# Moving the pair sums of a two-layer attention kernel to GpSimd, with a larger share of the subtraction on VectorE and the subtraction one group later

## The chip, the cores and the metric

The kernel runs on one core of a Trainium2 chip. The metric is the device time of one execution in microseconds (us).

## The reference

A float32 image of 2 x 512 x 48 x 48 goes through two layers, each an attention with a residual. Layer 0 normalises in 32 groups first and has biases; layer 1 adds a position embedding to the input of queries and keys. Both have 8 heads of 64 channels over 2304 positions:

```python
scores = jnp.einsum('bhqd,bhkd->bhqk', q, k) * scale
attn = jax.nn.softmax(scores, axis=-1)
o = jnp.einsum('bhqk,bhkd->bhqd', attn, v)
o = o.transpose(0, 2, 1, 3).reshape(B, S, HEADS * hd_v)
o = o @ Wout + bout
```

## The kernel before

The program is written as raw queues: each engine has its own list of instructions, and semaphores order them. The stages follow each other: group norm, projections of layer 0, attention of layer 0, output projection and projections of layer 1, attention of layer 1, output projection. The change touches `attention_stage` alone, which runs once per layer.

An attention stage has NB = 48 blocks: 2 images x 4 pairs of heads x 6 chunks of 384 queries. A block has 18 key tiles of 128 keys, in KC = 6 groups of three, c = 0 to 5. Every engine runs the same software pipeline: `body(t, par)` walks the six steps of block t, and in step c each engine also does work for earlier groups. `behind(t, par, c, lag)` gives the block and group that lie `lag` steps back.

What happens to a group, in steps after its scores:
- TensorE, `scores` (L681): scores of both heads for each of the three key tiles, into three pairs of PSUM banks (k = 0, 1, 2). `bank_free` waits until ScalarE has copied the bank's last contents.
- VectorE, `maximum` (L860): running maximum over the key tiles, from PSUM and a running buffer. ScalarE, `copy` (L755): the scores from PSUM into `prob`, after the maximum. After step 5 VectorE folds the two running maxima (`fold_slots`, L866).
- In step 0 of the next block TensorE transposes the fold (`turn`, L651), VectorE reduces it (L847), and in step 1 TensorE broadcasts the maxima (L658) and ScalarE copies them to `mx` (L763).
- Lag 7, `shift` (L589): `prob - mx`, columns 0 to 207 of 384 on VectorE, 208 to 383 on GpSimd. GpSimd waits for VectorE's part of the same group.
- Lag 9, `exponential` (L771) on ScalarE, two instructions for the two heads, after both parts.
- Lag 10, `weigh` (L692): TensorE multiplies the exponentials with the values, into bank 6. Lag 10 too, `pair_tiles` (L872): VectorE adds two of the three key tiles of a group into `two_tiles`, so that the key sums need fewer products.
- Lag 11, `add_keys` (L708): TensorE sums over the keys with a matrix of ones, into bank 7, from `two_tiles` and the third tile.
- Then, for a finished block: ScalarE copies the weighted sums in step 3 (`copy_weighted`, L777) and the denominators in step 5 (`copy_den`, L783), TensorE transposes the denominators in step 2 of the next block (`turn_den`, L665), VectorE sums and inverts them (L889, L895), ScalarE widens (L789), TensorE spreads them in step 3 (L671), VectorE multiplies (`norm`, L905) and ScalarE's queue stores.

On TensorE's queue a step is: transposes if the step has any, scores, `weigh`, `add_keys`. On VectorE's: three maxima with what is interleaved, the fold, the pair, the subtraction. On ScalarE's: three copies, two exponentials with what is interleaved. GpSimd has its part of the subtraction alone. For the last block of a stage VectorE subtracts all 384 columns and the key sums take all three tiles.

Of the kernel before, what the change touches and what calls it, by code (L numbers as in the profile page):

```python
# [6 lines left out]
ALU = mybir.AluOpType  # L7
# [18 lines left out]
SCALE = float(D) ** -0.5  # L26
GN_EPS = 1e-5
NORM_STEPS = 10
SHIFT_DVE = 208
SHIFT_LAG, EXP_LAG, PV_LAG, PAIR_LAG, DEN_LAG = 7, 9, 10, 10, 11  # L30
TURN_AT, BROADCAST_AT = 0, 1
PV_COPY_AT, DEN_COPY_AT, DEN_TURN_AT, DEN_SPREAD_AT, STORE_AT = 3, 5, 2, 3, 3


def is_block(t, *numbers):
# [478 lines left out]
def attention_stage(nc, name, psum, bufs, qk_d, v_d, att_d, next_loads):  # L514
# [6 lines left out]
    with ExitStack() as ctx:  # L521
        def sem(n):
            return ctx.enter_context(nc.semaphore(f"{name}_{n}"))
# [17 lines left out]
        dve_shifted, pool_shifted = sem("dve_shifted"), sem("pool_shifted")  # L541
        exp_done = sem("exp_done")
        paired = sem("paired")
        pv_done = sem("pv_done")
        den_copied, pv_copied = sem("den_copied"), sem("pv_copied")
        den_turned, den_summed, inverted = sem("den_turned"), sem("den_summed"), sem("inverted")
        widened, spread = sem("widened"), sem("spread")
# [83 lines left out]
        def _(pe):  # L631
# [3 lines left out]
            def bank_free(t, c, k):  # L635
                if c > 0 or not before(t, 1):
                    pe.wait_ge(copied, slot(t, 3 * (c - 1) + k) if live(t) else slot(NB - 1, KT - 1))
                if c == BROADCAST_AT + 1 and not before(t, 1) and live(t - 1):
                    pe.wait_ge(mx_ready, 3 * (t - 1) + k + 1)

            def spare_free(t, c):
                if c == DEN_TURN_AT + 1 and not before(t, 3) and live(t - 3):
# [42 lines left out]
            def weigh(t, par, c):  # L685
                if c == 0 and not before(t, 1):
                    pe.wait_ge(pv_copied, t)
                pe.wait_ge(v_in[c], 16 * (t // JB + 1))
                pe.wait_ge(exp_done, 2 * group(t, c))
                for kt in range(3 * c, 3 * c + 3):  # L690
                    for d in range(0, P, 32):
                        mm = nc.tensor.matmul(psum[d:d + 32, 6, 0:CH], vst[:, kt, d:d + 32],  # L692
                                              prob[par][:, d // D, kt, :], start=(kt == 0), stop=(kt == KT - 1),
                                              tile_position=(0, d))
                return mm

            def add_keys(t, par, c):
                if c == 0 and not before(t, 1):
                    pe.wait_ge(den_copied, t)
                if last(t):  # L700
                    rounds = [[prob[par][:, e, 3 * c + i, :] for e in range(2) for i in tiles] for tiles in ((0, 1), (2,))]
                else:
                    pe.wait_ge(paired, group(t, c))
                    rounds = [[x for e in range(2) for x in (two_tiles[c % 2][:, e, :], prob[par][:, e, 3 * c + 2, :])]]
                for n, tiles in enumerate(rounds):
                    for i, tile in enumerate(tiles):
                        r = i * P // len(tiles)
                        mm = nc.tensor.matmul(psum[r:r + 32, 7, 0:CH], ones[:, :], tile, start=(c == 0 and n == 0),  # L708
                                              stop=(c == KC - 1 and (n == len(rounds) - 1 or r % D > 0)), tile_position=(0, r))
                return mm  # L710

            def body(t, par):
                for c in range(KC):
                    spare_free(t, c)
                    if c == TURN_AT and not before(t, 1) and live(t - 1):
                        bank_free(t, c, 2)
                        turn(t - 1)
                    if c == BROADCAST_AT and not before(t, 1) and live(t - 1):
                        bank_free(t, c, 2)
                        broadcast_max(t - 1)  # L720
                    if c == DEN_TURN_AT and not before(t, 3) and live(t - 3):
                        bank_free(t, c, 2)
                        turn_den(t - 3)
                    if c == DEN_SPREAD_AT and not before(t, 3) and live(t - 3):
                        bank_free(t, c, 2)
                        spread_den(t - 3)
                    if live(t):
                        for k in range(3):
                            bank_free(t, c, k)
                            scores(t, par, c, k)  # L730
                    tv, pv, cv = behind(t, par, c, PV_LAG)
                    td, pd, cd = behind(t, par, c, DEN_LAG)
                    mm = None
                    if live(tv):
                        mm = weigh(tv, pv, cv)
                    if live(td):
                        mm = add_keys(td, pd, cd)
                    if mm is not None:
                        mm.then_inc(pv_done, 1)

            blocks(pe, body)

# [1 line left out]
        def _(act):  # L744
            def copy(t, par, s):
                c, k = divmod(s, 3)
                if s < 2:
                    act.wait_ge(scored, scored_count(slot(t, s)))
                else:
                    act.wait_ge(maxed, maxed_count(t, s))  # L750
                if c == TURN_AT and not before(t, 1):
                    act.wait_ge(reduced, 3 * (t - 1) + k + 1)
                if not before(t, 2):
                    act.wait_ge(pv_done, pv_count(t - 2, c + 1))
                nc.scalar.activation(prob[par][:, :, s, :], s_banks(k)[:, :, 0:CH], ACT.Copy).then_inc(copied, 1)  # L755

            def copy_max(t, par, r):
# [13 lines left out]
                nc.scalar.activation(x, x, ACT.Exp, scale=SCALE).then_inc(exp_done, 1)  # L771

            def copy_weighted(t):
                act.wait_ge(pv_done, pv_count(t, KC - 1))
                if not before(t, 1):
                    act.wait_ge(normed, 3 * t)
                nc.scalar.activation(pvr[:, :], pv_bank, ACT.Copy).then_inc(pv_copied, 1)  # L777

            def copy_den(t):
                act.wait_ge(pv_done, pv_count(t, KC))  # L780
                if not before(t, 1):
                    act.wait_ge(den_turned, t)
                nc.scalar.activation(den[:, :], den_bank, ACT.Copy).then_inc(den_copied, 1)  # L783
# [16 lines left out]
            def body(t, par):  # L800
                for c in range(KC):
                    te, pe_, ce = behind(t, par, c, EXP_LAG)
                    if c == DEN_COPY_AT and not before(t, 2) and live(t - 2):
                        copy_den(t - 2)
                    for k in range(3):
                        if k == 2 and c == DEN_TURN_AT and not before(t, 3) and live(t - 3):
                            widen(t - 3)
                        if live(t):
                            copy(t, par, 3 * c + k)
                        if c == BROADCAST_AT and not before(t, 1) and live(t - 1):  # L810
                            copy_max(t - 1, 1 - par, k)
                    for e in range(2):
                        if live(te):
                            exponential(te, pe_, ce, e)
                        if e == 0 and c == PV_COPY_AT and not before(t, 2) and live(t - 2):
                            copy_weighted(t - 2)
                    if c == STORE_AT and not before(t, 3) and live(t - 3):
                        store(t - 3, 1 - par)

# [3 lines left out]

        @block.gpsimd
        def _(pool):
            def body(t, par):
                for c in range(KC):
                    if c == 0:
# [1 line left out]
                    pool.wait_ge(copied, slot(t, 3 * c + 2))  # L830
                    pool.wait_ge(dve_shifted, group(t, c))
                    shift_part(nc.gpsimd, par, c, SHIFT_DVE, CH).then_inc(pool_shifted, 1)

            with pool.Fori(0, NB // 2 - 1) as it:
                for par in range(2):
                    body(2 * it + par, par)
            body(NB - 2, 0)

        @block.vector
        def _(dve):  # L840
# [21 lines left out]
            def fold_slots(t):  # L862
# [1 line left out]
                if not before(t, 1):  # L864
                    dve.wait_ge(turned, t)
                nc.vector.tensor_tensor(fold[:, :, :], run[0][:, :, :], run[1][:, :, :], ALU.max).then_inc(folded, 1)  # L866

            def pair_tiles(t, par, c):
                dve.wait_ge(exp_done, 2 * group(t, c))
                if c >= 2 or not before(t, 1):  # L870
                    dve.wait_ge(pv_done, pv_count(t, c - 1))
                nc.vector.tensor_tensor(two_tiles[c % 2][:, :, :], prob[par][:, :, 3 * c, :],  # L872
                                        prob[par][:, :, 3 * c + 1, :], ALU.add).then_inc(paired, 1)

            def shift(t, par, c):
                if c == 0:
# [30 lines left out]
            def body(t, par):  # L907
                for c in range(KC):
# [10 lines left out]
                            maximum(t, par, 3 * c + k)  # L919
                    if c == KC - 1 and live(t):  # L920
                        fold_slots(t)
                    tp, pp, cp = behind(t, par, c, PAIR_LAG)
                    if live(tp) and not last(tp):
                        pair_tiles(tp, pp, cp)
                    ts, ps, cs = behind(t, par, c, SHIFT_LAG)
                    if live(ts):
                        shift(ts, ps, cs)
# [171 lines left out]
```

## Time and profile before

| | |
|---|---|
| median of 3 runs | 4300.96 us (4295.68 to 4301.03) |
| profiled execution, its own time | 4301.96 us |
| its span, first to last instruction | 4300.2 us |
| granted TensorE clock, mean | 0.992 |
| TensorE busy with products | 4097.7 us (95%) |
| VectorE busy | 3211.7 us (75%) |
| ScalarE busy | 2815.7 us (65%) |
| GpSimd busy | 1408.7 us (33%) |
| DMA, mean over the span | 48 GB/s |

The busy times are of the whole span, which has four stages without attention work in it; within the attention stages VectorE and ScalarE are busier than these shares say. Matmuls are pipelined and their ends are modelled, so a busy TensorE may still have rests between steps. The clock is in parts of full speed.

### The profile page before, as it was taken

The page shows a single profiled execution, that of the slowest core. Times are in us where ns is not written, and L with a number is a line of the kernel's source. Part 1 is how long each engine was busy: PE and PEld are TensorE (multiplying, and loading weights), DVE is VectorE, ACT ScalarE, POOL GpSimd, SP SyncE. Part 2 cuts the span into 40 slices and gives each one's busy share as a digit, 9 for nine tenths or more (in the row PEclk, how much of TensorE's full clock was granted, in tenths as well). Part 3 has the DMA queues.
Part 4 walks back from the last instruction along what each step waited for, and adds up shares of the span by engine and source line. Part 5 has one row for each costly group of instructions (what it writes and reads, how often), then busy time and mean ns, then how long its engine had stood idle before and what let it go on. Part 6 is the DMA issues. An engine that isn't in the chain of part 4 may idle for free. (4 is left out here: it accounts for less than half of the span.)

```text
span 4300.2 us, 88739 instructions
## 1 busy us (share of the span) xinstructions
PE 4097.7 (95%) x30024; PEld 1912.0 (44%) x30024; DVE 3211.7 (75%) x4032; ACT 2815.7 (65%) x3557; POOL 1408.7 (33%) x572
## 2 busy tenths in 40 slices
PE   7998999999999999998999989999999999999989
PEld 4554444444444444444555544444444444444445
DVE  3112899999999999997322239999999999999962
ACT  1112788888888888886000018888888888888850
POOL 0000444444444444443100004444444444444410
PEclk9999999999999999999999999999999999999999
DMA  4122000101000000011323320100000000000116
GB/s 173 73 80 86 8 28 18 35 13 31 21 26 22 22 24 24 26 48 41 124 101 124 105 84 9 35 15 31 18 27 24 22 22 24 26 20 29 41 45 212
DMA packets 157934, 208.42 MB, mean 48 GB/s; under 512 B 9009, under 2 KB 144305, under 8 KB 156849
## 3 DMA queue, kind: packets, MB, share of 16 engines
q1 hardware_dynamic: 137712, 179.28, 12.7%
q10 hardware_dynamic: 20160, 28.32, 1.8%
q8 instruction: 39, 0.64, 0.1%
q14 instruction: 23, 0.18, 0.0%
HBM read 113.19 MB, written 94.37 MB: 48 GB/s over the span
## 5 line engine op out<-in xcount | busy, mean ns | idle before, releaser
L589 POOL TENSOR_TENSOR prob<-prob,mx 128x1056 f32<-128x1056 f32 x564 | 1387.7, 2460 | 2675.9 <-DVE prob L589 2675.9
L755 ACT ACTIVATE prob<-psum_att 128x768 f32<-128x768 f32 x1728 | 1393.3, 814 | 967.9 <-PE psum_att L681 539.4
L681 PE MATMUL psum_att<-qst,kst 64*128 64x384 f32 x6912 | 1288.3, 504 | 26.8 <-DMA kst<-qk_scratch 17.9
L692 PE MATMUL psum_att<-prob,vst 128*32 128x384 f32 x13824 | 1239.9, 491 | 77.3 <-ACT prob L771 77.2
L771 ACT ACTIVATE prob<-prob 128x1152 f32<-128x1152 f32 x1152 | 1285.6, 1164 | 0.0
L860 DVE TENSOR_TENSOR run<-psum_att,run 128x768 f32<-128x768 f32 x1344 | 1234.0, 950 | 11.9 <-PE psum_att L681 2.7
L589 DVE TENSOR_TENSOR prob<-prob,mx 128x1248 f32<-128x1248 f32 (+1 forms) x576 | 853.5, 1483 | 65.4 <-ACT mx L763 65.4
L681 PEld LDWEIGHTS psum_att<-qst,kst 64*128 64x128 f32 x6912 | 624.0, 188 | 530.7 <-ACT prob L755 152.3
L692 PEld LDWEIGHTS psum_att<-prob,vst 128*32 128x32 f32 x13824 | 396.1, 109 | 834.9 <-issue 573.3
L872 DVE TENSOR_TENSOR two_tiles<-prob 128x768 f32<-128x768 f32 x564 | 559.0, 991 | 0.4 <-ACT prob L771 0.4
L309 PE MATMUL psum<-xc_l,wq 128*128 128x384 f32 x1536 | 504.0, 489 | 10.1 <-DVE qk_l L406 5.0
L708 PE MATMUL psum_att<-prob,const_sb 128*32 128x384 f32 x2400 | 483.5, 487 | 0.0
L708 PE MATMUL psum_att<-two_tiles,const_sb 128*32 128x384 f32 x2256 | 465.0, 487 | 0.0
L309 PEld LDWEIGHTS psum<-xc_l,wq 128*128 128x128 f32 x1536 | 293.8, 191 | 220.9 <-issue 20.3
L860 DVE TENSOR_TENSOR run<-psum_att,prob 128x768 f32<-128x768 f32 x192 | 183.6, 957 | 100.4 <-PE psum_att L681 100.4
L350 ACT ACTIVATE qk_l<-psum,par_sb 128x384 f32<-128x384 f32 x96 | 55.7, 580 | 309.1 <-PE psum L309 309.1
L176 PE MATMUL psum<-attc_l,wo_l 128*128 128x384 f32 x768 | 252.5, 490 | 3.3 <-PEq L521 3.3
L424 DVE TENSOR_TENSOR vo_l<-psum,bv 128x512 f32<-128x512 f32 x36 | 24.9, 692 | 308.5 <-PE psum L326 308.5
L708 PEld LDWEIGHTS psum_att<-two_tiles,const_sb 128*32 128x32 f32 x2256 | 140.4, 110 | 217.2 <-issue 217.2
L176 PEld LDWEIGHTS psum<-attc_l,wo_l 128*128 128x128 f32 x768 | 147.2, 192 | 106.0 <-issue 5.8
L406 DVE TENSOR_TENSOR qk_l<-psum,emb_table 128x384 f32<-128x384 f32 x96 | 53.2, 557 | 187.2 <-PE psum L309 187.2
L708 PEld LDWEIGHTS psum_att<-prob,const_sb 128*32 128x32 f32 x2400 | 146.9, 110 | 8.2 <-issue 7.7
(55 smaller groups left out, 1596.3 us busy)
## 6 DMA issues: line engine op xcount, KB each, us to landing
qk_scratch<-qk_l SPq DMA_DIRECT2D x48, 768.0 KB, 3.5
v_scratch<-vo_l SPq DMA_DIRECT2D x24, 768.0 KB, 3.5
qst<-qk_scratch SPq DMA_DIRECT2D x96, 192.0 KB, 2.4
kst<-qk_scratch SPq DMA_DIRECT2D x96, 192.0 KB, 2.4
vst<-v_scratch SPq DMA_DIRECT2D x96, 192.0 KB, 2.5
att_scratch<-ob ACTq DMA_DIRECT2D x96, 192.0 KB, 1.9
attc_l<-att_scratch SPq DMA_DIRECT2D x24, 768.0 KB, 5.4
x_sb<-in_x SPq DMA_DIRECT2D x8, 1152.0 KB, 13.9
```

The costliest lines, as they stand in the source:

```text
L176: mm = nc.tensor.matmul(bank, w[c], att[:, c, :], start=(c == 0), stop=(c == CT - 1))
L309: mm = nc.tensor.matmul(qk_bank(m), qkv["w"][:, c, m * P:(m + 1) * P], xc[p][:, c, :], start=(c == 0), stop=(c == CT - 1))
L350: nc.scalar.activation(qk[half][:, mt, :], qk_bank(m), ACT.Identity, bias=bias[:, m:m + 1])\
L406: nc.vector.tensor_tensor(qk[half][:, mt, :], qk_bank(m), emb_of(i, m), ALU.add)\
L589: return engine.tensor_tensor(x, x, m, ALU.subtract)
L681: mm = nc.tensor.matmul(psum[:, 2 * k + e, 0:CH], kst[rows, (3 * c + k) * P:(3 * c + k + 1) * P], qst[par][rows, :], start=True, stop=True ...
L692: mm = nc.tensor.matmul(psum[d:d + 32, 6, 0:CH], vst[:, kt, d:d + 32], prob[par][:, d // D, kt, :], start=(kt == 0), stop=(kt == KT - 1), ...
L708: mm = nc.tensor.matmul(psum[r:r + 32, 7, 0:CH], ones[:, :], tile, start=(c == 0 and n == 0), stop=(c == KC - 1 and (n == len(rounds) - 1 ...
L755: nc.scalar.activation(prob[par][:, :, s, :], s_banks(k)[:, :, 0:CH], ACT.Copy).then_inc(copied, 1)
L771: nc.scalar.activation(x, x, ACT.Exp, scale=SCALE).then_inc(exp_done, 1)
L860: nc.vector.tensor_tensor(r[:, :, :], s_banks(s % 3)[:, :, 0:CH], other, ALU.max).then_inc(maxed, 1)
L872: nc.vector.tensor_tensor(two_tiles[c % 2][:, :, :], prob[par][:, :, 3 * c, :], prob[par][:, :, 3 * c + 1, :], ALU.add).then_inc(paired, 1)
```

## The change

Constants: VectorE's share of the subtraction goes from 208 to 304 of 384 columns, GpSimd's from 176 to 80. The subtraction is 8 steps behind the scores instead of 7, `weigh` 11 instead of 10, `add_keys` stays at 11, the exponential at 9 and the pair at 10. The finished block's steps move: both copies to step 4, the transpose of the denominators to 3, the spread and the store to 4. `pair_tiles` goes from VectorE's queue to GpSimd's, behind the subtraction of the same step (which is of the group two later); it still waits for the exponentials and for the key sums that last read its buffer. `weigh` has a semaphore of its own, so that the weighted sums can be copied before the key sums of that step.

```diff
-SHIFT_DVE = 208
-SHIFT_LAG, EXP_LAG, PV_LAG, PAIR_LAG, DEN_LAG = 7, 9, 10, 10, 11
+SHIFT_DVE = 304
+SHIFT_LAG, EXP_LAG, PAIR_LAG, PV_LAG = 8, 9, 10, 11
 TURN_AT, BROADCAST_AT = 0, 1
-PV_COPY_AT, DEN_COPY_AT, DEN_TURN_AT, DEN_SPREAD_AT, STORE_AT = 3, 5, 2, 3, 3
+PV_COPY_AT, DEN_TURN_AT, DEN_SPREAD_AT, STORE_AT = 4, 3, 4, 4
...
+                if c > BROADCAST_AT + 1 and not live(t) and live(t - 1):
+                    pe.wait_ge(mx_ready, 3 * t)
...
-                return mm
+                if c == KC - 1:
+                    mm.then_inc(weighed, 1)
...
-                return mm
+                mm.then_inc(pv_done, 1)
...
                     tv, pv, cv = behind(t, par, c, PV_LAG)
-                    td, pd, cd = behind(t, par, c, DEN_LAG)
-                    mm = None
                     if live(tv):
-                        mm = weigh(tv, pv, cv)
-                    if live(td):
-                        mm = add_keys(td, pd, cd)
-                    if mm is not None:
-                        mm.then_inc(pv_done, 1)
+                        weigh(tv, pv, cv)
+                        add_keys(tv, pv, cv)
...
                 if not before(t, 2):
-                    act.wait_ge(pv_done, pv_count(t - 2, c + 1))
+                    act.wait_ge(pv_done, pv_count(t - 2, c))
...
             def copy_weighted(t):
-                act.wait_ge(pv_done, pv_count(t, KC - 1))
+                act.wait_ge(weighed, t + 1)
...
             def copy_den(t):
-                act.wait_ge(pv_done, pv_count(t, KC))
+                act.wait_ge(pv_done, pv_count(t, KC - 1))
...
-                    if c == DEN_COPY_AT and not before(t, 2) and live(t - 2):
-                        copy_den(t - 2)
...
                         if e == 0 and c == PV_COPY_AT and not before(t, 2) and live(t - 2):
                             copy_weighted(t - 2)
+                    if c == PV_COPY_AT and not before(t, 2) and live(t - 2):
+                        copy_den(t - 2)
...
         @block.gpsimd
         def _(pool):
+            def pair_tiles(t, par, c):
+                pool.wait_ge(exp_done, 2 * group(t, c))
+                if c >= 2 or not before(t, 1):
+                    pool.wait_ge(pv_done, pv_count(t, c - 2))
+                nc.gpsimd.tensor_tensor(two_tiles[c % 2][:, :, :], prob[par][:, :, 3 * c, :],
+                                        prob[par][:, :, 3 * c + 1, :], ALU.add).then_inc(paired, 1)
+
...
                     shift_part(nc.gpsimd, par, c, SHIFT_DVE, CH).then_inc(pool_shifted, 1)
-
-            with pool.Fori(0, NB // 2 - 1) as it:
-                for par in range(2):
-                    body(2 * it + par, par)
-            body(NB - 2, 0)
+                    tp, pp, cp = behind(t, par, c, PAIR_LAG - SHIFT_LAG)
+                    if live(tp):
+                        pair_tiles(tp, pp, cp)
+
+            body(0, 0)
+            with pool.Fori(0, (NB - 2) // 2) as it:
+                for p in range(2):
+                    body(2 * it + 1 + p, 1 - p)
+            for c in range(KC - PAIR_LAG + SHIFT_LAG, KC):
+                pair_tiles(NB - 2, 0, c)
...
-            def pair_tiles(t, par, c):
-                dve.wait_ge(exp_done, 2 * group(t, c))
-                if c >= 2 or not before(t, 1):
-                    dve.wait_ge(pv_done, pv_count(t, c - 1))
-                nc.vector.tensor_tensor(two_tiles[c % 2][:, :, :], prob[par][:, :, 3 * c, :],
-                                        prob[par][:, :, 3 * c + 1, :], ALU.add).then_inc(paired, 1)
...
-                    tp, pp, cp = behind(t, par, c, PAIR_LAG)
-                    if live(tp) and not last(tp):
-                        pair_tiles(tp, pp, cp)
```

## Rows read from the trace of the kernel before

**Rows 1.** Window 500 to 1950: busy of PE, PEld, DVE, ACT, POOL; clock.
```profile
500.00:1950.00 1450.00, 1399.19 (x12378) 612.81 (x12372) 1360.02 (x1668) 1259.09 (x1582) 646.80 (x263) 1.00 0.08 26
```

**Rows 2.** Waits, 1000 to 1900: us in total, times, longest.
```profile
PE psum_att L692 <- ACT prob L771: 19.1, 27, 0.7
```

**Rows 3.** Timeline of TensorE, one block (steps 2, 3, 4, 5, 0, 1).
```profile
1002.87 2.21 PE L681 MATMUL psum_att<-qst,kst 64*128 64x384 f32 x12
...
1006.97 0.49 PE L708 MATMUL psum_att<-two_tiles,const_sb 128*32 128x384 f32 x1
...
1007.88 0.55 PE L671 MATMUL psum_att<-const_sb,dwide 128*128 128x128 f32 x3
1008.36 2.21 PE L681 MATMUL psum_att<-qst,kst 64*128 64x384 f32 x12
...
1013.22 2.21 PE L681 MATMUL psum_att<-qst,kst 64*128 64x384 f32 x12
1016.13 2.14 PE L692 MATMUL psum_att<-prob,vst 128*32 128x384 f32 x24 [0.71 <-ACT prob L771]
1018.85 2.21 PE L681 MATMUL psum_att<-qst,kst 64*128 64x384 f32 x12
...
1023.73 0.85 PE L651 MATMUL psum_att<-const_sb,fold 128*128 128x128 f32 x6
1024.51 2.21 PE L681 MATMUL psum_att<-qst,kst 64*128 64x384 f32 x12
...
1030.16 2.21 PE L681 MATMUL psum_att<-qst,kst 64*128 64x384 f32 x12
...
1035.45 0.55 PE L665 MATMUL psum_att<-const_sb,den 128*128 128x128 f32 x3 [0.37 <-ACT mx L763]
1035.93 2.21 PE L681 MATMUL psum_att<-qst,kst 64*128 64x384 f32 x12
```

**Rows 4.** Timeline of VectorE in the same block: a subtraction, pairs, the fold.
```profile
1002.47 1.46 DVE L589 TENSOR_TENSOR prob<-prob,mx 128x1248 f32<-128x1248 f32 x1 [0.69 <-ACT mx L763]
...
1006.90 0.95 DVE L872 TENSOR_TENSOR two_tiles<-prob 128x768 f32<-128x768 f32 x1
...
1012.67 0.95 DVE L872 TENSOR_TENSOR two_tiles<-prob 128x768 f32<-128x768 f32 x1
...
1022.62 0.96 DVE L866 TENSOR_TENSOR fold<-run 128x768 f32<-128x768 f32 x1
...
1027.98 1.19 DVE L872 TENSOR_TENSOR two_tiles<-prob 128x768 f32<-128x768 f32 x1
...
1033.88 0.95 DVE L872 TENSOR_TENSOR two_tiles<-prob 128x768 f32<-128x768 f32 x1
```

**Rows 5.** Timeline of ScalarE in the same block: copies, and the den copy.
```profile
1007.02 0.81 ACT L755 ACTIVATE prob<-psum_att 128x768 f32<-128x768 f32 x1
...
1012.78 0.81 ACT L755 ACTIVATE prob<-psum_att 128x768 f32<-128x768 f32 x1 [0.25 <-DVE run L860]
...
1015.97 2.46 ACT L755 ACTIVATE prob<-psum_att 128x768 f32<-128x768 f32 x3
...
1020.43 0.48 ACT L783 ACTIVATE den<-psum_att 128x384 f32<-128x384 f32 x1
```

**Rows 6.** Groups by line and form, 700 to 2000, and one instruction of GpSimd.
```profile
L589 POOL TENSOR_TENSOR prob<-prob,mx 128x1056 f32<-128x1056 f32 x235 | 578.2, 2460 | 716.1 <-DVE prob L589 716.1
...
L589 DVE TENSOR_TENSOR prob<-prob,mx 128x1248 f32<-128x1248 f32 x235 | 341.2, 1452 | 26.9 <-ACT mx L763 26.9
...
1004.01 2.47 POOL L589 TENSOR_TENSOR prob<-prob,mx 128x1056 f32<-128x1056 f32 x1 [4.01 <-DVE prob L589]
```

**Rows 7.** Both engines at once: timeline; the table sum's min/median/max ns.
```profile
4121.79 2.47 POOL L589 TENSOR_TENSOR prob<-prob,mx 128x1056 f32<-128x1056 f32 x1 [3.53 <-DVE prob L589]
4122.56 2.52 DVE L872 TENSOR_TENSOR two_tiles<-prob 128x768 f32<-128x768 f32 x1
...
L228 POOL TENSOR_TENSOR emb_table<-emb_parts x4: 4047/5208/6429, 2036.9 to 2051.4; 128x2304 f32<-128x2304 f32 x4
```

More of the change, by code:

```diff
@@ L543, in attention_stage @@
         paired = sem("paired")
-        pv_done = sem("pv_done")
+        weighed, pv_done = sem("weighed"), sem("pv_done")
         den_copied, pv_copied = sem("den_copied"), sem("pv_copied")
```

## The prediction

> **What bounds the kernel now.** I read the busy windows first, then the waits, then the timelines of one block on all engines. Over a steady attention stretch TensorE is busy 1399 of 1450 us, VectorE 1360, ScalarE 1259, GpSimd 647, at a granted clock of 1.00 [rows 1]. TensorE sets the pace, with VectorE close behind, and its products stand still in two places only, once a block each: 27 times 0.7 for the exponential in 900 us [rows 2], and 0.37 behind the copy of the maximum [rows 3]. The reader should see that the most to be won is TensorE's rest, not VectorE's work.
>
> A block has six steps c = 0 to 5 and takes 33.06 us (1035.93 - 1002.87) [rows 3]. A step without anything extra takes 4.86 (1008.36 to 1013.22). The key sums of a step begin 4.10 after its scores (1006.97 - 1002.87). The transposes add 0.48 (den turn), 0.48 (spread), 0.78 (turn) and 0.79 (broadcast: 5.65 from 1024.51 to 1030.16, less 4.86), together 2.53. So TensorE needs 6 x 4.86 + 2.53 = 31.69, and 1.37 is waiting: 0.43 before the den turn (1035.45 against 1030.16 + 4.86), 0.15 before the spread (1007.88 against 1007.73), 0.77 in step 4, whose value products wait for the second exponential, and 0.02 before the turn. There are 45 such blocks a layer (I count 45 even intervals between the turns), 90 in all: the waiting is worth 90 x 1.37 = 123 us and no more.
>
> **The change part by part.**
> Subtraction a step later, value products a step later (lag 11). The exponential of a group is then two steps old when its products come; the 0.77 goes. What is late next in that place is the copy of the weighted sums, which had ended 0.28 before the weigh would have wanted it. The den turn moves from step 2 to step 3: it no longer follows the three copies of the maximum, which ended just before it, and the copies of step 2 have no widening or den sums among them. The 0.43 goes. VectorE's wait for the maximum (0.69 a block [rows 4]) goes too, but VectorE was not the bound there. The spread and the three normalisations move from step 3 to 4, behind the widening in step 3: I take the same 0.15 for the spread as now (its bank's last copy starts 4.15 after the step's start and ends at 4.96 [rows 5]; spread at 5.01).
>
> ScalarE, steps 4 and 5. Both copies, weighted and den, now fall into step 4, together with the normalisations that make its copies late. By today's step 3: the third copy starts 4.42 after the step's start (1012.78 - 1008.36); from there to the next step's first copy are 3.19 (copy, exponential, weighted copy, exponential), then 0.48 for the den copy that today comes a step later, then three copies in 2.46 [rows 5]. They end at 10.55, the turn can go at 10.60, and TensorE would want it at 9.72. New wait: 0.88. So part of what was won is lost one step later, before the turn.
>
> VectorE. 768 elements take 0.95 and 1248 take 1.45 [rows 4, 6], a slope of 1.05 ns and 0.15 fixed. The subtraction of 304 columns has 1824 elements: 1.45 + 576 x 1.05 = 2.05, 0.60 more. The pair, 0.87 from start to start, goes. VectorE wins 0.27 a step; nothing on the path gains by it, as TensorE is the pace.
>
> GpSimd. It subtracts 80 columns (480 elements) and adds pairs (768). The only row like it is 1056 elements in 2.46 [rows 6]. With a fixed part f, both together take P = 2.91 + 0.82 f. Bounds: f = 0 gives 2.91 (if the plain pair went at the rate of the embedding table's sum, 4.05 for 2304 [rows 7], P would be 2.47); a line through 1056 in 2.46 and 2304 in 4.05 gives f = 1.1 and P = 3.82. I take f = 0.15, as VectorE's own, P = 3.03: the nearest row is the subtraction itself, the table's sum has another pattern.
>
> The exclusion between the two. A VectorE operation with both inputs in SBUF doesn't run beside GpSimd: one pair addition that began 1.70 before the end of GpSimd's subtraction took 2.52 instead of 0.95, 1.57 more, while the table sum took GpSimd 6.43 instead of 4.05 where VectorE was first [rows 7]. So I charge the overlap less 0.13. The maxima, with an input in PSUM, stay at 0.95 beside GpSimd. The Trainium skill says the same (SBUF — State Buffer, "Who interferes with whom": a VectorE instruction with two SBUF inputs contends with a GpSimd one that reads SBUF, and the second blocks until the first is done); the trace agrees, 1.57 for 1.70, and it speaks against giving GpSimd more. In this kernel it matters now: GpSimd starts 0.08 after the subtraction ends (1004.01 for 1003.93 [rows 4, 6]), and the next one begins 2.6 later at the earliest.
>
> The new chain: subtraction of step c, GpSimd's part, its pair, then the key sums of step c+1, which stand before the next scores on TensorE's queue, so every delay there is TensorE's. Pairs are ready 2.05 + 0.08 + P + 0.06 = 2.19 + P after the subtraction's start. Its place after a step's start is where the pair stands today: 3.72 in step 1, 4.03 with den sums, 4.31 with normalisations, 3.47 in step 0 [rows 3, 4].
> - Step 2's sums: wanted at 4.86 + 4.10 = 8.96 from step 1's start, ready at 5.91 + P: late from P = 3.05.
> - Step 3's: the subtraction of step 2 starts at 8.59, is held 0.03, pairs at 13.84, wanted at 14.30. Step 4's: ready at S3 + 4.03 + 5.22 = 9.25, wanted at 5.49 + 4.10 = 9.59. Both in time.
> - Step 5's: ready at 4.31 + 5.22 = 9.53 from step 4's start, wanted at 8.96: 0.57 late, but within the 0.88 of ScalarE's copies. The fold (two SBUF inputs) stands at 8.89, is held by the pair to end at 7.27 + P = 10.30: also within it. Up to P = 3.28 this costs nothing more.
> - Step 0's: that subtraction starts at S4 + 7.19 + P, pairs ready at 2P - 2.00 after step 0's start, wanted at 4.10: late from P = 3.05, by twice the excess. The subtraction of step 0 is held about 0.4, which the next step takes up.
>
> Sum, P = 3.03: step 1 4.86; step 2 with den turn 5.34; step 3 to 4 5.01 + 0.48 = 5.49; to the turn 10.60 and 0.78; step 0 with broadcast 5.65: 32.72, against 33.06. 0.34 x 90 = 31 us. Fill and drain change by one step in which VectorE sets the pace; I put them at 0, within 5 us either way. The profiled execution is 4301.96 (span 4300.2 and 1.8 around it), 1.0 over the median 4300.96: 4301 - 31 = 4270.
>
> **The rivals.**
> Slower: GpSimd is dearer. Above 3.05 the block grows by 3 (P - 3.05), so it is even at P = 3.16, f = 0.31, only 0.13 over my value. With the table sum's rate as slope (1.76 ns), f = 0.60 and P = 3.40: 1.05 + 0.12 (step 5) more, 33.89, +0.83 x 90 = 75 us: 4376. At P = 3.82 the block is about 35.6: 4530. For it: no row shows GpSimd's fixed part, and the one other size is cheaper per element, as with a large f. Against: its pattern repeats both operands.
>
> No change: P between 3.12 and 3.20 (f 0.25 to 0.35), where the gain of 31 and the lateness of the pairs cancel; at 3.14 the block is 32.99, 6 us won: 4295. The GpSimd page of the skill (GPSIMD Engine Reference, "Elementwise — side-by-side cycle accounting") gives 4497 ns for 2048 elements; a line through that and the row's 2460 would give just this P, an estimate, and so 4295; no run here shows that size.
>
> All waiting gone: if the copies of steps 4 and 5 fit (VectorE 0.27 a step earlier, den copy behind other waits), 31.69 a block, 4301 - 123 = 4178; half of it 4225. Against: ScalarE's chain is made of operations back to back.
>
> **How the numbers follow.** Forecast 0.50 (4262 to 4285), more gained 0.08, no change 0.12, slower 0.30. Within 0.2% is about what a measurement can't tell from no change. Faster 0.58, same 0.12, slower 0.30. The range 4225 to 4395 goes from half the waiting gone to a little over the slope case, leaving 0.05 below and 0.13 above.
>
> **What would show it.** After the change: block 32.7; no wait of the value products for the exponential in step 4 and of the den turn; a wait of 0.8 to 0.9 before the turn, put down to ScalarE's copy; POOL 1.20 and 1.83; VectorE's subtraction 2.05, about 2.5 in step 0 and the fold about 1.4. TensorE waiting for GpSimd's pair in steps 0 and 2 would be the slower rival. The prediction is wrong if GpSimd's two take over 3.16, if the lock lets VectorE in between them, or if a drain grows by more than 5 us.

## The result and the profile after

The changed kernel takes 4267.54 us (median of 4, 4265.96 to 4270.81) against 4300.66 before: ratio 0.9927, 95% interval 0.9909 to 0.9944, 33 us less. The forecast was 4270.

The lines have moved in the changed kernel: scores L683, value products L694, key sums L711, turn L653, broadcast L660, den turn L667, spread L673, maximum L870, fold L876, GpSimd's pair L828, ScalarE's copies L753.

Busy windows of the changed kernel, the same stretch as in [rows 1] and the same columns:

```profile
500.00:1950.00 1450.00, 1425.85 (x12546) 608.52 (x12542) 1342.85 (x1424) 1253.63 (x1602) 801.79 (x535) 1.00 0.08 25
```

TensorE is now busy 1426 of 1450 us instead of 1399, GpSimd 802 instead of 647, VectorE 17 us less. The reader should see that the gain is TensorE's rest and no more. By these windows it is 27 us of it; by the length of the blocks below it is 0.44 x 44.5 = 20, and as the ends of products are modelled, the blocks are the better measure.

Waits of the changed kernel, 1000 to 1900 (total, times, longest):

```profile
PEld psum_att L711 <- POOL two_tiles L828: 40.5, 111, 0.6
...
PE psum_att L711 <- POOL two_tiles L828: 12.8, 28, 0.5
```

The two waits of before, for the exponential (27 times 0.7, [rows 2]) and behind the maximum's copy, are not there. One new one is: the key sums wait 0.46 for GpSimd's pair, once a block (PE is the products, PEld the loading of their weights). It shows in the timeline (TensorE, steps 4, 5, 0, 1, 2, 3 and the next 4; compare [rows 3]):

```profile
1001.95 2.21 PE L683 MATMUL psum_att<-qst,kst 64*128 64x384 f32 x12
...
1006.81 2.21 PE L683 MATMUL psum_att<-qst,kst 64*128 64x384 f32 x12
1008.94 2.14 PE L694 MATMUL psum_att<-prob,vst 128*32 128x384 f32 x24
1011.54 0.48 PE L711 MATMUL psum_att<-two_tiles,const_sb 128*32 128x384 f32 x1 [0.46 <-POOL two_tiles L828]
...
1012.36 0.85 PE L653 MATMUL psum_att<-const_sb,fold 128*128 128x128 f32 x6
1013.14 2.21 PE L683 MATMUL psum_att<-qst,kst 64*128 64x384 f32 x12
...
1017.31 0.51 PE L711 MATMUL psum_att<-two_tiles,const_sb 128*32 128x384 f32 x1
...
1018.89 2.21 PE L683 MATMUL psum_att<-qst,kst 64*128 64x384 f32 x12
...
1023.75 2.21 PE L683 MATMUL psum_att<-qst,kst 64*128 64x384 f32 x12
...
1029.08 2.21 PE L683 MATMUL psum_att<-qst,kst 64*128 64x384 f32 x12
...
1034.09 0.55 PE L673 MATMUL psum_att<-const_sb,dwide 128*128 128x128 f32 x3
1034.57 2.21 PE L683 MATMUL psum_att<-qst,kst 64*128 64x384 f32 x12
```

The block is 32.62 (1034.57 - 1001.95) where it was 33.06. Step by step against the prediction: step 4 to the turn 10.41 (10.60 predicted), turn 0.78 (0.78), step 0 5.75 (5.65), step 1 4.86 (4.86), step 2 with den turn 5.33 (5.34), step 3 with spread 5.49 (5.49). The waits are 0.69 before the turn, 0.15 before the spread and 0.10 in step 0: 0.93 instead of 1.37.

This is layer 0. In layer 1 every second block of the changed kernel is 0.11 longer (32.72 and 32.61 in turn): the third maximum of its step 3 starts 0.21 after the reciprocal and not 0.11 (3021.63 after 3021.42, 3054.24 after 3054.13), and the copy and the spread behind it are as late. The kernel before and the version with the lags alone don't have it, every version with the later lags and the pairs on GpSimd does. Its cause stays open; it is worth some 2 us.

VectorE, GpSimd and ScalarE in step 5 of the same block (compare [rows 4, 5]):

```profile
1008.22 2.68 DVE L870 TENSOR_TENSOR run<-psum_att,run 128x768 f32<-128x768 f32 x3
1010.94 1.27 DVE L876 TENSOR_TENSOR fold<-run 128x768 f32<-128x768 f32 x1
1012.14 2.04 DVE L589 TENSOR_TENSOR prob<-prob,mx 128x1824 f32<-128x1824 f32 x1
...
1008.38 1.22 POOL L589 TENSOR_TENSOR prob<-prob,mx 128x480 f32<-128x480 f32 x1 [2.76 <-DVE prob L589]
1009.55 1.84 POOL L828 TENSOR_TENSOR two_tiles<-prob 128x768 f32<-128x768 f32 x1
...
1009.56 0.49 ACT L781 ACTIVATE den<-psum_att 128x384 f32<-128x384 f32 x1
1009.93 2.22 ACT L753 ACTIVATE prob<-psum_att 128x768 f32<-128x768 f32 x3
```

The pair ends at 1011.39, the key sums begin at 1011.54 (wanted at 1006.81 + 4.10 = 1010.91) and the turn follows them 0.82 later. The last copy ends at 1012.15, the fold, held by the pair, at 1012.21, and the turn stands at 1012.36. Which of the three is last? In all ten profiles of this case the turn stands 0.14 or 0.15 behind the end of the fold, whatever the key sums and the copies do. Late key sums in other steps (vector_256, move_only) are followed by the next transposes after 0.78 to 0.79, and the spread stands 0.05 behind the end of its bank's copy. By these the key sums would allow the turn at 1012.32 and the copies at 1012.20. So the fold is last, the key sums 0.04 and the copies 0.16 before it, and the fold and the key sums both hang on the end of GpSimd's pair.

The groups by form, 700 to 1950 (compare [rows 6]):

```profile
L589 DVE TENSOR_TENSOR prob<-prob,mx 128x1824 f32<-128x1824 f32 x230 | 500.1, 2174 | 0.0
...
L828 POOL TENSOR_TENSOR two_tiles<-prob 128x768 f32<-128x768 f32 x231 | 425.2, 1841 | 0.0
L589 POOL TENSOR_TENSOR prob<-prob,mx 128x480 f32<-128x480 f32 x230 | 278.1, 1209 | 558.2 <-DVE prob L589 558.2
...
L876 DVE TENSOR_TENSOR fold<-run 128x768 f32<-128x768 f32 x38 | 48.5, 1277 | 1.3
```

GpSimd's two take 1.21 and 1.84; as the second starts 1.17 after the first, P is 3.01. VectorE's subtraction is 2.05 at the median (2.05 + 0.12 on average, what the exclusion costs it), the fold 1.28 instead of 0.96.

### The profile page after: what moved, and what is told of

It is laid out like the page before. It is cut to its first block and busy times, and to the rows that moved or that the text cites. A ratio compares the mean times of both kernels' runs of the same rounds, so it can differ in the third digit from the quotient of the medians.

```text
span 4264.2 us, 88501 instructions
## 1 busy us (share of the span) xinstructions
PE 4117.6 (97%) x30024; PEld 1882.8 (44%) x30024; DVE 3141.5 (74%) x3468; ACT 2773.2 (65%) x3557; POOL 1727.9 (41%) x1136
## 5 line engine op out<-in xcount | busy, mean ns | idle before, releaser
L753 ACT ACTIVATE prob<-psum_att 128x768 f32<-128x768 f32 x1728 | 1360.7, 822 | 970.9 <-PE psum_att L683 559.3
L589 POOL TENSOR_TENSOR prob<-prob,mx 128x480 f32<-128x480 f32 x564 | 690.0, 1223 | 2335.8 <-DVE prob L589 2335.8
L683 PE MATMUL psum_att<-qst,kst 64*128 64x384 f32 x6912 | 1288.8, 505 | 29.6 <-DMA kst<-qk_scratch 17.8
L870 DVE TENSOR_TENSOR run<-psum_att,run 128x768 f32<-128x768 f32 x1344 | 1234.3, 950 | 56.7 <-PE psum_att L683 42.8
L589 DVE TENSOR_TENSOR prob<-prob,mx 128x1824 f32<-128x1824 f32 (+1 forms) x576 | 1264.4, 2196 | 3.6 <-ACT mx L761 3.6
L694 PE MATMUL psum_att<-prob,vst 128*32 128x384 f32 x13824 | 1241.6, 491 | 0.4 <-issue 0.4
L828 POOL TENSOR_TENSOR two_tiles<-prob 128x768 f32<-128x768 f32 x564 | 1041.2, 1846 | 0.0
L683 PEld LDWEIGHTS psum_att<-qst,kst 64*128 64x128 f32 x6912 | 623.4, 188 | 533.7 <-ACT prob L753 101.8
L694 PEld LDWEIGHTS psum_att<-prob,vst 128*32 128x32 f32 x13824 | 394.1, 109 | 754.3 <-issue 702.7
L711 PE MATMUL psum_att<-two_tiles,const_sb 128*32 128x384 f32 x2256 | 469.0, 490 | 51.9 <-POOL two_tiles L828 51.8
L711 PE MATMUL psum_att<-prob,const_sb 128*32 128x384 f32 x2400 | 490.4, 491 | 0.0
L870 DVE TENSOR_TENSOR run<-psum_att,prob 128x768 f32<-128x768 f32 x192 | 182.8, 953 | 108.6 <-PE psum_att L683 108.6
L711 PEld LDWEIGHTS psum_att<-two_tiles,const_sb 128*32 128x32 f32 x2256 | 115.0, 109 | 325.8 <-issue 174.8
L857 DVE TENSOR_REDUCE mcol<-psum_att 128x2 f32<-128x256 f32 x288 | 122.0, 425 | 44.9 <-PE psum_att L683 38.7
```

The lines of the kernel that those rows point to most:

```text
L589: return engine.tensor_tensor(x, x, m, ALU.subtract)
L683: mm = nc.tensor.matmul(psum[:, 2 * k + e, 0:CH], kst[rows, (3 * c + k) * P:(3 * c + k + 1) * P], qst[par][rows, :], start=True, stop=True ...
L828: nc.gpsimd.tensor_tensor(two_tiles[c % 2][:, :, :], prob[par][:, :, 3 * c, :], prob[par][:, :, 3 * c + 1, :], ALU.add).then_inc(paired, 1)
L857: nc.vector.tensor_reduce(mcol[:, :, r], s_banks(r)[:, :, CH:512], AX.X, ALU.max).then_inc(reduced, 1)
L870: nc.vector.tensor_tensor(r[:, :, :], s_banks(s % 3)[:, :, 0:CH], other, ALU.max).then_inc(maxed, 1)
```

## The experiments

The two theories: (1) what was won is TensorE's two waits, by the later value products and the later den turn, and the move of the pairs to GpSimd is a cost; (2) what was won is VectorE's relief. All times below are medians of 4 with the ratio to the kernel before on the same chip (it took 4300.28 and 4299.69 us beside the two sets of runs).

**lags_only.** The changed kernel, the pairs back on VectorE ahead of its subtraction, 208 columns.

```diff
-SHIFT_DVE = 304
+SHIFT_DVE = 208
...
-                    if live(tp):
-                        pair_tiles(tp, pp, cp)      # on GpSimd
...
+                    tp, pp, cp = behind(t, par, c, PAIR_LAG)
+                    if live(tp) and not last(tp):
+                        pair_tiles(tp, pp, cp)      # on VectorE
```

> The later subtraction, value products, copies and den turn alone; pairs stay on VectorE and the subtraction at 208 columns. Theory 1 (the gain is the later value products and den turn, 0.77 and 0.43 us a block; the move to GpSimd is a cost): a block of 32.3 to 32.4 us, only the spread's 0.15 and about 0.5 before the turn left as waits; 4240 us, faster than the changed kernel's 4268. Theory 2 (the gain is VectorE's relief): nothing much won, 4290 to 4301.

Measured 4244.28 (4243.20 to 4245.75), ratio 0.987 [0.9853, 0.9886]. Half the change is faster than the whole. TensorE's timeline, a turn, step 4's scores and the next turn; and VectorE's fold:

```profile
1009.98 0.85 PE L653 MATMUL psum_att<-const_sb,fold 128*128 128x128 f32 x6 [0.58 <-DVE fold L864]
...
1032.08 2.21 PE L683 MATMUL psum_att<-qst,kst 64*128 64x384 f32 x12
...
1042.44 0.85 PE L653 MATMUL psum_att<-const_sb,fold 128*128 128x128 f32 x6 [0.58 <-DVE fold L864]
...
1041.33 0.96 DVE L864 TENSOR_TENSOR fold<-run 128x768 f32<-128x768 f32 x1
```

The block is 32.46 (1042.44 - 1009.98). Here the turn stands 10.36 after step 4's start and waits for the fold: VectorE, with the pair, sets that place. No key sums wait. Theory 1 holds; theory 2 falls.

This also prices the move to GpSimd. The fold starts 9.25 after step 4's start here (1041.33 - 1032.08) and 8.99 in the changed kernel: VectorE's relief makes it 0.26 earlier. But there the pair holds it for 0.31, and step 0 is 0.10 longer: 0.16 a block in all. Of the 21.0 us between the two profiled spans 16.7 lie between the even turns, layer 1's longer blocks included; the other 4.3 are in fill and drain.

**move_only.** The other half: the kernel before with `SHIFT_DVE = 304` and the pairs on GpSimd's queue, three steps behind its subtraction, all lags and places as before.

```diff
-SHIFT_DVE = 208
+SHIFT_DVE = 304
...
+                    tp, pp, cp = behind(t, par, c, PAIR_LAG - SHIFT_LAG)
+                    if live(tp):
+                        pair_tiles(tp, pp, cp)      # on GpSimd, PAIR_LAG 10, SHIFT_LAG 7
...
-                    tp, pp, cp = behind(t, par, c, PAIR_LAG)
-                    if live(tp) and not last(tp):
-                        pair_tiles(tp, pp, cp)      # on VectorE
```

> The other half: pairs on GpSimd and 304 columns on VectorE, all lags and places as in the kernel before. Theory 1: the three waits of the kernel before stay, and the key sums of step 2 come late by some 0.7 us, as the subtraction of the step before waits for the maximum; a block of 33.7, 4355 us, slower than before. Theory 2: 4265 to 4280, as VectorE has 0.27 us a step less to do.

Measured 4368.99 (4368.02 to 4370.02), ratio 1.0159 [1.0142, 1.0176]. Its TensorE timeline (lines as in the kernel before) has the old waits and a new one; the block is 33.76 (1037.08 - 1003.32):

```profile
1003.32 0.85 PE L651 MATMUL psum_att<-const_sb,fold 128*128 128x128 f32 x6
...
1015.15 0.55 PE L665 MATMUL psum_att<-const_sb,den 128*128 128x128 f32 x3 [0.37 <-ACT mx L763]
...
1020.41 0.51 PE L708 MATMUL psum_att<-two_tiles,const_sb 128*32 128x384 f32 x1 [0.51 <-POOL two_tiles L830]
...
1029.44 2.14 PE L692 MATMUL psum_att<-prob,vst 128*32 128x384 f32 x24 [0.71 <-ACT prob L771]
...
1037.08 0.85 PE L651 MATMUL psum_att<-const_sb,fold 128*128 128x128 f32 x6
```

The key sums of step 2 stand 0.68 late, as expected, and the block is 0.70 longer; that is 63 of the 69 us, and the time is 14 above the 4355 expected.

The two halves, -56 and +69 us, don't add up to -33, which is 46 less than their sum. Here VectorE's subtraction waits 1.56 for the maximum once a block (27 times between 1000 and 1900, 42.0 us), and that makes the pair late in step 2; with the later subtraction that wait is gone. The lags are worth more where the pairs are on GpSimd.

**vector_336.** The changed kernel with `SHIFT_DVE = 336`.

> The changed kernel with 336 columns on VectorE instead of 304: VectorE's subtraction 2.25 instead of 2.05, GpSimd's 0.80 instead of 1.21, the chain from the subtraction's start to the pair 0.2 shorter. Theory 1 (the pair sets the wait before the turn): that wait falls from 0.69 to 0.5, the 0.10 of step 0 goes; a block of 32.33, 4242 us. Rival (ScalarE's copies set it, as predicted): 4266 to 4275, as VectorE's longer subtraction only makes the copies later.

Measured 4246.71 (4243.76 to 4248.69), ratio 0.9877 [0.9861, 0.9894]. **vector_320**, `SHIFT_DVE = 320`:

> The changed kernel with 320 columns on VectorE. Theory 1: at 304 the key sums set the turn (10.4 after step 4's start), at 336 sums, fold and copies come within 0.1 of each other; at 320 the pair is late by 0.45 in step 5 and the fold is held by 0.16; a block of 32.42 us, between the two, 4250 us.

Measured 4244.94 (4243.72 to 4248.19), ratio 0.9875 [0.9858, 0.9891]. The two are the same within their spread (blocks of 32.40 and 32.39); 320 was not between 304 and 336. TensorE, GpSimd, ScalarE and VectorE of vector_336 about the turn (its step 4 begins at 1030.45):

```profile
1039.85 0.48 PE L711 MATMUL psum_att<-two_tiles,const_sb 128*32 128x384 f32 x1 [0.26 <-POOL two_tiles L828]
...
1040.73 0.85 PE L653 MATMUL psum_att<-const_sb,fold 128*128 128x128 f32 x6
...
1037.08 0.82 POOL L589 TENSOR_TENSOR prob<-prob,mx 128x288 f32<-128x288 f32 x1 [3.16 <-DVE prob L589]
1037.85 1.85 POOL L828 TENSOR_TENSOR two_tiles<-prob 128x768 f32<-128x768 f32 x1
...
1038.42 2.22 ACT L753 ACTIVATE prob<-psum_att 128x768 f32<-128x768 f32 x3
...
1039.63 0.96 DVE L876 TENSOR_TENSOR fold<-run 128x768 f32<-128x768 f32 x1
```

The key sums wait 0.26 instead of 0.46, the fold is no longer held (0.96), the turn stands at 10.28 instead of 10.41, and the block is 32.38 (1040.73 - 1008.35, the turn before). Of the 0.24 a block, 0.13 is the wait before the turn and the rest step 0's key sums, which are in time again. The copies end at 10.19, where they ended in the changed kernel (10.20), so they did not set the turn there: the rival falls. But VectorE's longer subtraction does cost. The fold starts at 9.18 instead of 8.99, and only because the pair no longer holds it does it end earlier, at 10.14 instead of 10.26, 0.14 before the turn. The copies are now 0.09 before the turn, so little more can be won here by shortening the pair's chain alone.

**vector_256.** The same dial the other way, `SHIFT_DVE = 256`.

> The changed kernel with 256 columns on VectorE: VectorE's subtraction 1.75 instead of 2.05, GpSimd's 1.84 instead of 1.21, the chain to the pair 0.33 longer. Theory 1 (the chain from the subtraction to the key sums is the price, three times a block): late by 0.3 in step 2, by 0.9 in step 5 instead of 0.63, by 0.5 in step 0 instead of 0.1: a block of 33.6 us instead of 32.62, 4355 us. Rival (VectorE's own work is what counts): 0.3 a step less on VectorE, 4240 to 4265 us.

Measured 4356.43 (4353.76 to 4358.23), ratio 1.0133 [1.0116, 1.015]. The key sums are late in all three places named, and the fold is held longest (TensorE's timeline, step 0, step 2, step 5 and the turn, then VectorE's fold):

```profile
1001.90 0.51 PE L711 MATMUL psum_att<-two_tiles,const_sb 128*32 128x384 f32 x1 [0.21 <-POOL two_tiles L828]
...
1012.73 0.51 PE L711 MATMUL psum_att<-two_tiles,const_sb 128*32 128x384 f32 x1
...
1029.37 0.48 PE L711 MATMUL psum_att<-two_tiles,const_sb 128*32 128x384 f32 x1 [0.77 <-POOL two_tiles L828]
...
1030.19 0.85 PE L653 MATMUL psum_att<-const_sb,fold 128*128 128x128 f32 x6
...
1028.15 1.89 DVE L876 TENSOR_TENSOR fold<-run 128x768 f32<-128x768 f32 x1
```

VectorE has 0.3 a step less to do and the kernel is 89 us slower. In step 2 the sums stand 4.40 after the step's start (1012.73 - 1008.33) instead of 4.10: 0.30 late, as expected. The block is 33.54 (turns at 1030.19 and 1063.73).

**pair_first.** The changed kernel, on GpSimd's queue the pair ahead of the subtraction of the same step.

```diff
             for c in range(KC):
+                    tp, pp, cp = behind(t, par, c, PAIR_LAG - SHIFT_LAG)
+                    if live(tp):
+                        pair_tiles(tp, pp, cp)
                     if c == 0:
                         pool.wait_ge(mx_ready, 3 * (t + 1))
```

> The changed kernel with GpSimd's pair ahead of its subtraction in each step, so that the pair is no longer behind VectorE's subtraction of the same step. Theory 1: no wait for the pair is left anywhere, but in step 5 the pair now stands beside the fold and holds it, to end about 10.35 after step 4's start: 0.10 to 0.15 a block won, 4255 us, and the wait before the turn falls to the fold. Rival (the exclusion of the two engines plays no part, the key sums were all): the wait before the turn falls to 0.5 and 4240 us.

Measured 4280.49 (4279.25 to 4281.02), ratio 0.9954 [0.9937, 0.997]: 13 us slower than the changed kernel, where I had expected 12 faster. TensorE, GpSimd and VectorE about the turn (step 4 begins at 1008.30):

```profile
1018.99 0.85 PE L653 MATMUL psum_att<-const_sb,fold 128*128 128x128 f32 x6 [0.91 <-DVE fold L876]
...
1016.18 1.84 POOL L828 TENSOR_TENSOR two_tiles<-prob 128x768 f32<-128x768 f32 x1 [0.23 <-ACT prob L769]
...
1017.29 1.55 DVE L876 TENSOR_TENSOR fold<-run 128x768 f32<-128x768 f32 x1
```

The key sums wait for nothing, as expected. But GpSimd's pair starts later in step 5 than I had taken (behind the exponential), lasts to 1018.02 and holds the fold by 0.59, where the expected end at 10.35 left room for 0.40. The turn stands at 10.69 instead of 10.41: 0.28 later, which is what the fold is held longer (0.59 for 0.31), while the key sums came in time. This is the second sign that in the changed kernel, too, the held fold sets the turn. The exclusion of the two engines alone costs more here than fold and late key sums together did there.

**lags_176.** lags_only with `SHIFT_DVE = 176`.

> The lags alone, with 176 instead of 208 columns on VectorE (the pairs too stay there). Theory 1: the fold sets the turn in the version with the lags alone (0.64 wait); VectorE's subtraction is 0.2 shorter (1.25), so the fold could begin 0.2 earlier, but GpSimd's part (2.87) now ends after that and holds it; 0 to 0.1 a block won, 4235 to 4245 us. Rival (no exclusion): the full 0.2, and with step 4's and step 5's parts together 0.3: 4217 us.

Measured 4243.44 (4243.12 to 4244.61), ratio 0.9869 [0.9853, 0.9886], no difference from lags_only. The fold and GpSimd's part beside it:

```profile
1008.46 1.16 DVE L864 TENSOR_TENSOR fold<-run 128x768 f32<-128x768 f32 x1
...
1005.90 2.90 POOL L589 TENSOR_TENSOR prob<-prob,mx 128x1248 f32<-128x1248 f32 x1 [2.90 <-DVE prob L589]
```

GpSimd's 2.90 ends at 1008.80, 0.34 into the fold, which is 0.20 longer: what VectorE saves on the subtraction the exclusion takes back.

**den_at_2.** lags_only with the den turn at step 2 and spread and store at 3.

```diff
-PV_COPY_AT, DEN_TURN_AT, DEN_SPREAD_AT, STORE_AT = 4, 3, 4, 4
+PV_COPY_AT, DEN_TURN_AT, DEN_SPREAD_AT, STORE_AT = 4, 2, 3, 3
```

> The lags alone, but the den turn left at step 2, spread and store at step 3, as in the kernel before. Theory 1 (0.43 of the gain is the den turn, which no longer stands behind the copy of the maximum): that wait is back, the wait for the exponential in step 4 stays away, and the fold is still 0.45 late; a block of 32.7 us instead of 32.46, 4267 us. Rival (the later value products are the whole gain): 4244 us or, with the normalisations a step further from the fold, less: 4230 us.

Measured 4280.45 (4279.96 to 4282.09), ratio 0.9956 [0.994, 0.9973]. TensorE's timeline:

```profile
1016.98 0.85 PE L653 MATMUL psum_att<-const_sb,fold 128*128 128x128 f32 x6 [0.55 <-DVE fold L864]
...
1028.70 0.55 PE L667 MATMUL psum_att<-const_sb,den 128*128 128x128 f32 x3 [0.36 <-ACT mx L761]
...
1049.84 0.84 PE L653 MATMUL psum_att<-const_sb,fold 128*128 128x128 f32 x6 [0.55 <-DVE fold L864]
```

The block is 32.86 (1049.84 - 1016.98): 0.40 more than lags_only, the den turn's wait and nothing else, as the wait before the turn stays at 0.62 although the normalisations are a step further from it (I had expected 0.45, and 4267 us). 32.86 against 33.06 is what the later subtraction, value products and copies leave without the later den turn: of their 0.77 they give back 0.6 to the fold. No run parts these three from each other.

## Why the prediction was right, and where it was not

The time: 4270 predicted, 4268 measured, and the block 32.72 against 32.62.

- **What bounds.** TensorE's rest of 1.37 was the most to be won, and it is what moved: 0.44 of it. Shown by the blocks, and by move_only and vector_256, where VectorE has less to do and the kernel is slower. But "nothing on the path gains by it" is too strong: once the two waits are gone, the fold at the end of VectorE's queue sets the turn, and VectorE's relief starts it 0.26 earlier than in lags_only.
- **The two waits removed** (0.77 and 0.43). Both are gone; den_at_2 brings 0.40 back with the den turn. The second is worth its full price. The first is not: most of it comes back before the turn, behind VectorE's fold, in lags_only by VectorE's own work and in the changed kernel because the pair holds it. The prediction had this as a new wait of 0.88; it is 0.69.
- **GpSimd's price.** P = 3.03 from VectorE's fixed part; measured 3.01 (1.21 and 1.84, less 0.04 that they overlap). The forms of all runs, 0.81 for 288 elements, 1.21 for 480, 1.84 for 768, 2.46 for 1056, 2.86 for 1248, lie on 2.14 ns an element and a fixed part of 0.19. The table's sum at 4.05 for 2304 is off that line; its operands repeat, but no run here shows that this makes it cheap. The rival with P = 3.14 was 0.13 too dear. It came from a line through the figure of the Trainium skill (GPSIMD Engine Reference, "Elementwise — side-by-side cycle accounting"). On the measured line 2048 elements would be 4.6, an estimate, near the 4.5 that the Trainium skill gives there.
- **The exclusion.** It cost what was charged, the overlap less 0.13: the fold is held by 0.45 - 0.14 = 0.31 (the pair ends 0.45 into it), 0.59 in pair_first, 0.20 in lags_176. The rule of the Trainium skill (SBUF — State Buffer, "Who interferes with whom") that the second blocks until the first is done agrees in each of them, but for these 0.13 to 0.14.
- **The step that failed: "They end at 10.55, the turn can go at 10.60".** ScalarE's chain in steps 4 and 5 was mis-sized: the copies end at 10.20 (1012.15 - 1001.95). The third copy of step 4 starts where it was put, at 4.43, and the 3.18 from there to the den copy are right too. But the den copy keeps ScalarE busy 0.37 from start to start, not 0.48, and the three copies take 2.22, not 2.46. The 2.46 was no duration of ScalarE: in the kernel before the last of these copies stood right behind the last maximum,

```profile
1014.90 2.68 DVE L860 TENSOR_TENSOR run<-psum_att,run 128x768 f32<-128x768 f32 x3
```

which ends at 1017.58, and the copy starts at 1017.62 (1015.97 + 2.46 - 0.81). In the changed kernel the last copy starts 0.44 after the last maximum. So the wait before the turn is not ScalarE's. It is the pair's, by way of the fold that it holds, with the key sums 0.04 before that, and the sentence that a late pair in step 5 "costs nothing more" up to P = 3.28 is wrong: it costs already at 3.01. pair_first shows that the fold counts, vector_336 that the copies did not.
- **How much of it was luck.** The fold was put to end at 10.30 and ends at 10.26; the turn follows it by 0.15, as in the kernel before (1023.73 after 1022.62 + 0.96). These terms give 10.45. The total came out because this next term lay only 0.15 below the wrong 10.60. The turn was forecast 0.19 too late and step 0 0.10 too short, and the two errors have opposite signs.
- **Step 0.** Pairs were to be ready at 4.06 and wanted at 4.10; the sums stand at 4.17 and the step is 0.10 longer. This follows from the same error: the subtraction was to start 0.38 before the turn (10.22 for 10.60) and starts 0.22 before it (10.19 for 10.41), so its pair comes 0.16 later after step 0's start. The threshold of 3.05 held only for a turn at 10.60.
- **Fill and drain.** Put at 0 within 5 us; the blocks give 36.2 us between the even turns of both layers in the two profiles (19.3 and 16.9, the second less because of layer 1's longer blocks) and the spans differ by 36.0. Beside these blocks the fill of layer 0 won 4.7 and the two drains lost 1.4 and 3.2 (from the last turn to the first product of the next stage, 55.15 for 53.71 and 52.68 for 49.53).

What stays open: whether the turn can be had earlier than 10.2 after step 4's start. The fold and ScalarE's copies both end at 10.14 to 10.19 in vector_336, so both would have to move; normalising after the maxima was not tried. Runs at 320 and 336 columns and with the lags alone all end between 4243 and 4247, the best here and all 21 to 24 us better than the changed kernel; which of pairs on VectorE or on GpSimd is better is not settled between them.

## What to carry to other kernels

When TensorE sets the pace, price a change by the waits of its queue, one by one, and ask for each which of the other things that the same instruction needs comes next; here the 0.77 won in step 4 ran into three other inputs of the turn, all 0.5 to 0.7 late and within 0.2 of each other, and the latest of those decides the gain. Before a duration is added into a chain, look whether the row contains a wait: 2.46 for three copies was VectorE's pace, ScalarE's own was 2.22. Work moved to GpSimd counts as a stage in a chain, not as a share of an idle engine: 33% busy said nothing of the 3.0 us that now lie between VectorE's subtraction and TensorE's sums. And try the parts of a change alone: the part with the smaller diff was worth 56 us, the whole 33.

## What the runs showed of the hardware that was not expected

GpSimd and a VectorE instruction with both inputs in SBUF take turns instruction by instruction, in both directions. VectorE's fold is held by what is left of GpSimd's pair, less 0.13 to 0.14 us. The other way round, GpSimd's sum of the embedding table started 2.51 us before the end of VectorE's (2036.95 for 2036.90 + 2.56, kernel before) and took 2.38 more (6.43 for 4.05), 0.13 less than the overlap. Three ScalarE copies of 128 x 768 take 2.22 us from first start to last end when each maximum has ended well before its copy, and 2.46 to 2.54 when they follow the maxima closely.

The key sums before the turn begin 0.14 to 0.15 us after the pair's end, those of other steps after 0.05 to 0.06 (1017.31 after 1015.42 + 1.83). It is not that they had waited: in move_only the key sums of step 2 waited 0.51 and began 0.05 after the pair. No term of the prediction had these 0.09, and their cause stays open.
